# A three-stage transformer-like layer on one core: the first stage's weight chain interleaved with the first pair's products, and the projection weights made in twelve portions

## What is computed

```python
q = einsum('bnf,nfd->bnd', flat, Wq) + bq        # flat (64,64,768), Wq (64,768,192); k, v alike
scores = einsum('bnd,cnd->nbc', q, k) / sqrt(192)
attn = einsum('nbc,cnd->bnd', softmax(scores), v)
att = layernorm(attn) * ln_g + ln_b + flat @ p1_w + p1_b
h = att @ w0 + b0;  h = h @ w1 + b1;  h = h @ w2 + b2;  h = h @ w3 + b3;  h = h @ w4 + b4
h = softmax(h + att @ p2_w + p2_b, axis=2)       # (64,64,192)
```

## Time and profile before

| | us |
|---|---|
| three timed runs | 1263.8, 1267.02, 1269.12 (median 1267.02) |
| the profiled execution | 1262.91, of it 1260.7 from the first to the last instruction (the span) |
| TensorE busy | 1169.6 (93%), mean granted clock 0.973 |
| DVE, ACT, POOL busy | 786.3 (62%), 722.8 (57%), 560.7 (44%) |
| bytes read from memory, written | 154.87 MB, 22.02 MB |

### The profile page before, as it was taken

How to read it: one execution, slowest core, us unless ns; L and a number is a source line. 1 busy time by engine, 2 the same in 40 slices (tenths; PEclk the granted TensorE clock), 3 DMA queues, 4 the chain that set the end, 5 groups by cost and what they waited for, 6 DMA issues and landing times.

```text
span 1260.7 us, 47618 instructions
## 1 busy us (share of the span) xinstructions
PE 1169.6 (93%) x18596; PEld 954.3 (76%) x18596; DVE 786.3 (62%) x2152; ACT 722.8 (57%) x1955; POOL 560.7 (44%) x690
## 2 busy tenths in 40 slices
PE   5899999999999558999999999999999999999975
PEld 5865666666666356888888888888888888888864
DVE  0027433333333335787888888887887887888862
ACT  0012222222222247788888888888888888888752
POOL 0000000000000046676776676776676776676631
PEclk8999999999999778999999999999999999999997
DMA  9979999999998001212222222222222222222220
GB/s 320 341 279 352 360 373 375 375 382 372 374 369 330 16 13 25 50 36 41 49 45 39 49 47 39 49 47 41 47 46 39 49 47 40 48 48 36 45 43 21
DMA packets 220196, 179.54 MB, mean 142 GB/s; under 512 B 164406, under 2 KB 190073, under 8 KB 219513
## 3 DMA queue, kind: packets, MB, share of 16 engines
q1 hardware_dynamic: 220010, 176.94, 45.2%
HBM read 154.87 MB, written 22.02 MB: 140 GB/s over the span
## 4 chain that ended last, share of the span: by engine, by line
POOL 36%; PE 31%; issue 23%; DVE 6%; SPq 2%; DMA 1%; ACT 1%; POOLq 0%; DVEq 0%; ACTq 0%
PE PS L443 28%; POOL region L1148 15%; POOL region L1131 6%; POOL region L1136 3%; POOL region L1142 2%; POOL region L1114 1%; POOL region L1098 1%; POOL region L1121 1%; POOL region L1107 1%; DVE region L1454 1%; PE PS L519 1%; SPq L312 1%; POOL region L1111 1%; POOL region L1100 1%; PE PS L537 1%
## 5 line engine op out<-in xcount | busy, mean ns | idle before, releaser
L443 PE MATMUL PS<-region 64*64 64x64 f32 (+6 forms) x5864 | 349.9, 284 | 20.7 <-DVE region L1196 12.2
L443 PEld LDWEIGHTS PS<-region 64*64 64x64 f32 (+3 forms) x5864 | 228.4, 137 | 120.4 <-issue 107.0
L1148 POOL TENSOR_TENSOR region<-region,powers 128x12 f32<-128x12 f32 x96 | 237.2, 2471 | 7.6 <-POOL region L1142 0.2
L1077 POOL TENSOR_TENSOR region<-region,powers 128x1 f32<-128x1 f32 x32 | 6.1, 189 | 404.0 <-DVE region L1256 404.0
L708 PE MATMUL PS<-region 64*64 64x64 f32 x4608 | 154.4, 220 | 2.3 <-ACT region L959 2.1
L708 PEld LDWEIGHTS PS<-region 64*64 64x64 f32 x4608 | 144.4, 134 | 14.9 <-issue 9.2
L443 PE MATMUL PS<-cw_hi,xr_hi 128*128 128x256 f32 (+3 forms) x384 | 145.5, 379 | 3.8 <-DVE xr_lo L1495 1.2
L926 ACT ACTIVATE region<-PS 128x512 f32<-128x512 f32 (+1 forms) x192 | 93.7, 489 | 77.6 <-PE PS L443 74.4
L443 PE MATMUL PS<-cw_lo,xr_hi 128*128 128x256 f32 (+3 forms) x384 | 130.6, 340 | 0.0
L443 PE MATMUL PS<-cw_hi,xr_lo 128*128 128x256 f32 (+3 forms) x384 | 130.4, 340 | 0.0
L849 ACT ACTIVATE region<-PS 128x384 f32<-128x384 f32 x32 | 15.7, 491 | 192.7 <-PE PS L443 192.7
(11 more groups left out here) (171 smaller groups left out, 2184.6 us busy)
## 6 DMA issues: line engine op xcount, KB each, us to landing
region<-in_Wq SPq DMA_DIRECT2D x32, 1152.0 KB, 5.9
region<-in_Wk SPq DMA_DIRECT2D x32, 1152.0 KB, 8.2
region<-in_Wv SPq DMA_DIRECT2D x32, 1152.0 KB, 8.0
region<-in_x SPq DMA_DIRECT2D x32, 384.0 KB, 6.9
n_scratch<-region SPq DMA_DIRECT2D x64, 192.0 KB, 3.5
region<-h_scratch SPq DMA_DIRECT2D x64, 96.0 KB, 3.1
region<-in_w SPq DMA_DIRECT2D x2, 2304.0 KB, 13.4
region<-i_scratch SPq DMA_DIRECT2D x256, 12.0 KB, 1.8
```

The source lines that it names most:

```text
L443: return nc.tensor.matmul(dst, lhsT, rhs, start=first, stop=last)
L1148: pool.tensor_tensor(rs[:, cols], rs_var[:, cols], root[:, cols], ALU.pow).then_inc(S["rs_ready"], 1)
```

## The change

It has these parts:

1. **The chain's first copy ahead of the small setup.** The chain's bias `chain_b` leaves the list of twenty small loads and is loaded ahead of `w2`, with a signal of its own. DVE does `chain_step(0)` (copy and add) before it waits for the nineteen others (`par_in`).
2. **The first pair's products inside the chain.** The q and k products of pair 0 stand between the chain's second and third product, its V products after the third, and its `p1` products after the small feed-forward products. The chain's outputs move to PSUM banks 5 to 7 for it. The loop begins with step 1. The wait for `eff_ready`, `ones_set` and `ffn_ready` moves into step 1 ahead of the transposes, and asks for 2 of the 7 `ffn_ready` signals; the rest is waited for before the second stage.
3. **Twelve portions.** `centre_weights` and `split_weights` work on 768 of the 2304 columns at a time, for the upper and the lower rows, in steps 3 to 14. The loop that DVE runs for the rest is written out further for it (16 steps ahead of the loop and not 8).
4. **Between the stages.** `spread_shift` and `fold_weights` move from iteration `s == 1` to the end of the first stage. POOL sets the five regions as soon as it has done the last pair; for this those regions change their place in memory, to lie over buffers of the chain and not over buffers of the pairs.

```diff
-                     (chain_b[:, :, :], d["chain_b"]), (p2a[:, :], d["p2"][0:HALF]), (p2b[:, :], d["p2"][HALF:ATT + 1]),
+                     (p2a[:, :], d["p2"][0:HALF]), (p2b[:, :], d["p2"][HALF:ATT + 1]),
...
+            sp.dma_start(chain_b[:, :, :], d["chain_b"]).then_inc(S["chain_b_in"], 16)
             sp.dma_start(chain_w[1][:, :, :], d["w2"]).then_inc(S["chain_in1"], 16)
...
             def chain_out(i):
-                return PS[:, i // 2, (i % 2) * (ATT + 1):(i % 2 + 1) * (ATT + 1)]
+                return PS[:, 5 + i // 2, (i % 2) * (ATT + 1):(i % 2 + 1) * (ATT + 1)]
...
+                if k == 1:
+                    pe.wait_ge(S["wx_in0"], 64)
+                    for c_ in range(CH):
+                        qk_chunk(first_pair, c_)
+                else:
+                    for c_ in range(CH):
+                        v_chunk(first_pair, c_)
...
-            pe.wait_ge(S["eff_ready"], 3)
-            pe.wait_ge(S["ones_set"], 1)
-            pe.wait_ge(S["ffn_ready"], 7)
+            pe.wait_ge(S["par_in"], 19 * 16)
+            for c_ in range(CH):
+                p1_chunk(first_pair, c_)
...
+                if t.known and t.n == 1:
+                    pe.wait_ge(S["eff_ready"], 3)
+                    pe.wait_ge(S["ones_set"], 1)
+                    pe.wait_ge(S["ffn_ready"], 2)
...
-            for s in range(2):
-                step_b(s // 2, s % 2)
+            step_b(0, 1)
...
+            pe.wait_ge(S["att_ready"], PAIRS)
+            pe.wait_ge(S["v_copied"], PAIRS)
+            pe.wait_ge(S["qkT_ready"], PAIRS)
+            pe.wait_ge(S["pt_copied"], PAIRS)
+            spread_shift()
+            pe.wait_ge(S["ffn_ready"], 7)
+            pe.wait_ge(S["cw_ready"], 6)
...
-                if s == 1:
-                    spread_shift()
...
-            pool.wait_ge(S["h_out0"], PAIRS // 2 * 32)
-            pool.wait_ge(S["h_out1"], PAIRS // 2 * 32)
+            pool.wait_ge(S["cw_ready"], 6)
...
+            chain_step(0)
+            dve.wait_ge(S["par_in"], 19 * 16)
...
+            def centre_weights(part):
+                k, m = divmod(part, 3)
+                cols = slice(m * KD, (m + 1) * KD)
...
-                if s.known and 2 <= s.n < 6:
-                    (centre_weights, split_weights)[s.n % 2]((s.n - 2) // 2)
-            pipeline(dve, PAIRS, 4, step_b_and_weights)
-            dve.wait_ge(S["region_ready"], 5)
+                if s.known and 3 <= s.n < 15:
+                    (split_weights, centre_weights)[s.n % 2]((s.n - 3) // 2)
+            pipeline(dve, PAIRS, 8, step_b_and_weights)
...
+            fold_weights()
+            dve.wait_ge(S["region_ready"], 6)
...
-                if s == 1:
-                    fold_weights()
```

More of the change, by code:

```diff
@@ L267, in build @@
         y2T1 = part("second", P, P)
-        y2T2 = part("second", P, P)
         f1 = part("second", P, P)
@@ L273, in build @@
         res = [part("second", P, ATT) for _ in range(2)]
+        x_aug = part("second", P, 4, P)
+        xg2 = part("second", R2 + 1, P)
+        y2T2 = part("second", P, P)
+        dT = part("second", P, HEADS, SEQ)
+        inv = part("second", NBLK * HEADS, BLK, BLK)
         xr_hi, xr_lo = [[sb(f"{name}{i}", [P, 4, P], F32R) for i in range(2)] for name in ("xr_hi", "xr_lo")]
@@ L543, in step_b @@
                     for c_ in range(3):
-                        v_chunk(c_)
+                        v_chunk(t, c_)
                 if old:
```

120 lines of the change are left out of this document (62 added, 58 removed).

## The result

The changed kernel takes 1255.16 us (median of 6 runs, 1251.66 to 1259.77) against 1266.8 us (6 runs, 1263.16 to 1269.33) of the kernel before: a ratio of 0.9914, 95% interval [0.9886, 0.9942], some 11.6 us less. Measured once more beside other runs it took 1256.2 (4 runs), ratio 0.991 [0.9893, 0.9926]. Forecast were 1250.7 and a gain of 16.3. The sign and the order of size are right, the range holds the time, and some 4.5 us are missing. The trace says more than the median: a load that the forecast took to be in time is 5.46 us late, and a row that I had before me pointed at it.

A forecast was written before the change was run, and what follows sets the result against it. TensorE's own work was taken to set the steady 11.06 us steps, with waits at the start and between the stages; 10.7 + 4.6 - 0.7 + 1.7 = 16.3 us gained, from 1267.0 to 1250.7 us, range 1243 to 1259.

The forecast's parts named there:

- The start: Kernel start up to pair 1: pair 1 begins at 65.0 instead of 75.7, a gain of 10.7 us.
- lands hardly earlier: Load of w3 for the chain's third product: issued earlier, yet still taken to land at 43.3.
- So it fits, by a margin of under 1 us: Pair 2's load, needed when step 1 ends: lands between 73 and 74, so step 2 doesn't wait for it.
- The portions: Twelve portions of weight work in the first stage's steps 3 to 14: hidden entirely, gain 4.6 us, bounds 3.6 and 4.6.
- the 3.5 us of hidden work: First-stage steps: at least 3.5 us of work like step 4's lower rows' piece hides in a step, so a portion hides.
- Between the stages and the fold: First stage's end to iteration 2 of the second: loss 0.7 us between the stages, gain 1.7 us from the moved fold.
- L676 without a fold: Second stage, iteration 2: transposes (L657 in the forecast) start at 469.65 instead of 471.40, a gain of 1.7 us.
- The second stage from there on is as long as before: Second stage behind its first L657 group: unchanged in length; the forecast is wrong if its iterations change in length.
- (a): Rival at the start: the clock falls in the wait for w3, costing 2.8 us; 13.5 gained, 1253.5 us; chance 0.23.
- (b): Rival in the first stage: the transfers set the pace, 10.7 us gained in place of 15.3; 1255.3 us; chance 0.12.
- (c): Rival: interleaving fails, w3 late or pair 2 not there; half the start's gain lost, 1256 to 1261 us; chance 0.10.
- (d): Rival, slower: two more POOL operations hit by DVE work in each second-stage iteration, costing 37.8 us; 1288.5 us; chance 0.05.

The follow-up runs named there:

- old_pieces: The changed kernel with the projection weights made as before, four whole pieces in steps 2 to 5: 1260.7 us (4 runs).
- cw_one: The changed kernel with the three cw loads laid out in memory as in the tile and loaded as one load of 128 full rows: 1251.6 us (4 runs).
- cw_late: The changed kernel with the ten loads of the second stage's weights issued behind pair 2's load and pair 1's biases: 1264.4 us (10 runs).
- rest_late: The changed kernel with only the seven small second-stage loads moved behind pair 1's biases, the three cw loads staying ahead: 1252.0 us (4 runs).
- cw_thirds: The changed kernel with each of the three cw loads cut into three loads of 768 columns: 1253.8 us (4 runs).
- after_again: The changed kernel itself, unchanged, measured and profiled once more: 1256.2 us (4 runs).
- fold_back: The changed kernel with the spreading matmuls and the fold of wo back in iteration 1 of the second stage: 1255.3 us (4 runs).

## Why the prediction was right, and where it was not

**The start: right.** 9.8 for 10.7. The 0.9 is `w3`, issued at 27.5 instead of 29.0 and landed at 44.4, not 43.3. The forecast that it "lands hardly earlier" was too mild: pair 0's input came 1.2 us late too, and q and k ran at the low clock (5.79 for 4.0), which the wait for `w3` hid.

**"So it fits, by a margin of under 1 us": this step failed.** The load of pair 2 was to land at 73 to 74 and landed at 80.9. I reckoned the loads ahead of it as "3.9 us of full work after 60" and pair 2 at 396 GB/s behind. Both come from rows 3, and rows 3 hold the warning: from 60 to 70 the share is 0.39 with 95 GB/s, so 95 / 0.39 = 244 GB/s at full share and not 396. That work was slow since 54 in the kernel before as well:

```profile
54.00:64.00 10.00, 8.25 (x51) 7.96 (x50) 1.73 (x3) 0.00 (x0) 0.00 (x0) 1.00 0.92 198
```

Before, it ran out beside TensorE's small products and hurt nobody; with the start 10 us earlier, pair 2's weights are in that stretch and go slow with it. And I took the sixteen engines as one: they leave the stretch unevenly, and the input is there only when the last of them has brought its part. The cost in the profile is 5.46 us of waiting, 1.4 us more at the low clock in step 2 and 0.6 behind it, some 7.5 in all.

**The portions: right.** No wait of TensorE for DVE in steps 3 to 14, 4.6 us forecast. The 4.0 of the table is that less the 0.6 of the low clock in step 2. `old_pieces` confirms it from the other side. One reading was wrong without consequence: the scaling stood in the piece of step 2, not in that of step 4; the 3.5 us of hidden work use only the two passes.

**Between the stages and the fold: right in the sum,** +1.0 forecast and measured. In parts: the memsets +0.3 (taken as 0, within the bound of 0.4), the fold -0.55 (forecast -0.7; `spread_shift` took 4.00 us, forecast 4.24), L676 without a fold +1.9 for 1.7. Not forecast: the drain of the last steps takes 0.7 us more. For 0.5 of it the clock falls earlier there (the `weff` group at 419.38 takes 1.44 for 0.92 us), and for 0.2 DVE is slower: L1298 takes 0.56 us beside a memset of POOL, and 0.37 to 0.38 in its 31 other steps. Whether this is the port pair that the forecast cited the Trainium skill for ("SBUF — State Buffer", Terms) is not shown; if it is, it costs 0.2 us here, not the 2.2 that all five memsets take.

**"The second stage from there on is as long as before": wrong in the profiles.** It takes 781.5 in the two profiles of kernels with the old start, 785.5 to 787.2 in all twelve that stem from the changed kernel. Over half lies in one interval: from the second to the third operation L1147, 23.5 us before, 26.4 to 26.6 in eight of the twelve, 24.9 to 25.2 in three, 23.65 in one (`cw_one`, which loses its 4 us further on). Another 1.7 us of after's 5.1 lie behind its last operation L1147 (54.6 us to the end, 52.9 before). Timeline of TensorE there, of after:

```profile
499.82 0.93 PE L717 MATMUL PS<-region 64*64 64x64 f32 x48 [1.01 <-DMA region<-i_scratch]
501.93 1.56 PE L717 MATMUL PS<-region 64*64 64x64 f32 x48 [1.18 <-issue]
...
505.00 6.13 PE L727 MATMUL PS<-region 64*64 64x64 f32 x144
```

The same two waits stand in the kernel before (0.87 and 1.18 us), where the last two groups took 0.93 and 4.80 us. So the clock falls at this place in one kernel and not in the other, with the same work and nearly the same waits. What decides it I can't show. Nor do I know whether the unprofiled executions have it: they lie 4 us above the profile in before and mostly below it in after, so the medians' gain (11.6) is larger than the profiles' (2.9). I don't count this as settled.

**The rivals.** (a) was the common case, not the forecast's no loss: of the nine profiles with this order of products seven took 19.90 to 21.17 us for the 18.27 of the group at `w3`, behind waits of 2.0 to 4.1 us, and only the first profile of after (1.79 us) and `cw_late` (2.01 us) kept 18.27. The most was in `rest_late`: a wait of 3.73 us, a clock of 0.66 from 40 to 50, 2.9 us for the 2.8 reckoned. In `cw_thirds` 2.01 us of waiting cost 1.7 us and in `cw_late` none, so I can give no limit. (b) was right that transfers set the pace, but in one step only, and by slow and uneven loads, not by lack of rate in the stage. Its 1255.3 is close to the measured time by chance. (c) said "or pair 2 isn't there", and that is what happened; in the profile 6.9 of the 9.8 us that the start had gained went in step 2. Its 1256 to 1261 holds the second median, 1256.2, and the first profiled execution, but not the first median. (d) didn't come: in the trace before and after iterations mostly take 23.6 us.

## What to carry to other kernels

Divide the rate by the share of the DMA engines before you reckon with either: here engines that were busy at half the rate meant loads for part of the partitions, and what was queued behind them paid. A load is there when the last engine has brought its part, not when the sum of the bytes would be. Lay such a tile out in memory so that one load fills all 128 partitions, even with spare rows, and look at the divisors of a load's row count. And moving one engine's work out of the way gains only if the next thing that is late is filled as well: the early copy alone gave nothing, with pair 0's products in the hole it gave 9.8 us.

## What I had not expected of the hardware

- Loads that reach 64 or 49 partitions: 192 to 228 GB/s at full share, 383 to 404 when the same tile is filled by a single load of 128 rows. A packet of 9216 bytes takes 353 ns for 128 partitions and 670 to 930 for these, and packets of other loads beside them up to 480 ns instead of 182.
- A load of 113 partitions: one engine, 26 GB/s; its last row was in at 97.8, those of the load of 128 rows ahead of it at about 56.
- The landing time of one load varies by 5 us between executions of the same start (77.6 to 82.6), with all engines at full share; the parts of it land up to 9 us apart.
- The clock after short waits: behind waits of 3.1 to 3.2 us ahead of pair 0's q and k these took 5.8 us (full clock: 4.1), behind 2.3 us 5.79 (`cw_one`), behind 2.0 us once 5.78 (`old_pieces`) and twice 4.09 (`after_again`, `fold_back`). Waits of this size can go either way.
